# Graph kernel on one Trainium2 core: the twelve weight halves of the edge stage are loaded later in the aggregation loop, and split into high and low behind it

## The reference

```python
# x: (10000, 512); src, dst: (5000,) with dst sorted; edge_attr: (5000, 512)
# layer 0: graph convolution with self loops
out = segment_sum((x @ W)[src] * norm, dst) + b      # norm = dinv[src] * dinv[dst]
x = layernorm(x + leaky_relu(out))
# layer 1: attention over edges
r = concat([x[src], x[dst], edge_attr]) @ Wr.T + br
q, k, v = (x @ Wq.T + bq)[dst], r @ Wk.T + bk, r @ Wv.T + bv
m = v * segment_softmax(sum(q * k) / 8, dst)          # 8 heads of 64
out = x + segment_sum(m, dst) @ Wo.T + bo
out = (out - mean) / sqrt(var + eps) * gamma + beta   # mean, var over the nodes
x = layernorm(x + out)
```

## Time and profile before

| | us |
|---|---|
| median of 3 runs | 1425.84 (1417.3 to 1426.75) |
| the profiled execution's own time | 1421.64 |
| its span in the trace | 1419.9 |
| mean granted clock of TensorE | 0.976 of full |

### The profile page before, as it was taken

One profiled execution on the slowest core, in us unless ns is written; L12 is line 12 of the kernel. 1 busy time (PEld: TensorE's weight loads), 2 busy tenths in 40 slices (PEclk: granted clock), 3 DMA queues, 4 the chain that ended last, 5 costly groups with the idle time before them and its releaser, 6 DMA issues. The chain is left out here.

```text
span 1419.9 us, 22043 instructions
## 1 busy us (share of the span) xinstructions
PE 1336.9 (94%) x6660; PEld 1074.2 (76%) x6660; DVE 1092.5 (77%) x2043; ACT 592.8 (42%) x1107; POOL 827.0 (58%) x762
## 2 busy tenths in 40 slices
PE   7798889999999979999999999999999999859997
PEld 6677778888787858888888888888888888634443
DVE  6476647888888723788888888888888888868787
ACT  3466644555555511322222222222222223246786
POOL 3455515666666533566665666666666665558785
PEclk9999999999999979999999999999999999879999
DMA  8688775666666351444444444444444444759855
GB/s 287 216 290 295 242 238 182 222 222 221 220 214 228 141 160 45 120 130 133 132 135 134 132 130 132 133 134 134 134 134 134 134 134 118 261 185 363 291 194 186
DMA packets 128302, 257.97 MB, mean 182 GB/s; under 512 B 21459, under 2 KB 21907, under 8 KB 128114
## 3 DMA queue, kind: packets, MB, share of 16 engines
q1 hardware_dynamic: 97490, 175.31, 37.7%
q0 software_dynamic: 29920, 80.38, 18.2%
q10 hardware_dynamic: 832, 1.57, 0.3%
HBM read 197.18 MB, written 73.60 MB: 191 GB/s over the span
## 5 line engine op out<-in xcount | busy, mean ns | idle before, releaser
L207 PE MATMUL ps<-w_lo,w_hi 128*128 128x512 f32 (+2 forms) x1140 | 414.9, 364 | 6.9 <-DVE w_lo L1456 4.2
L208 PE MATMUL ps<-w_hi,w_lo 128*128 128x512 f32 (+2 forms) x1140 | 409.9, 360 | 0.0
L209 PE MATMUL ps<-w_hi 128*128 128x512 f32 (+2 forms) x1140 | 409.4, 359 | 0.0
L207 PEld LDWEIGHTS ps<-w_lo,w_hi 128*128 128x128 f32 x1140 | 216.5, 190 | 39.3 <-DVE w_lo L1456 5.6
L209 PEld LDWEIGHTS ps<-w_hi 128*128 128x128 f32 x1140 | 216.4, 190 | 32.1
L208 PEld LDWEIGHTS ps<-w_hi,w_lo 128*128 128x128 f32 x1140 | 216.7, 190 | 29.8
L1240 POOL TENSOR_TENSOR acc_x<-acc_x,node_rows 128x512 f32<-128x512 f32 x72 | 115.2, 1600 | 79.7 <-DMA node_rows<-x_table 75.5
L918 POOL TENSOR_TENSOR node_y<-node_z,node_x 128x512 f32<-128x512 f32 x79 | 102.2, 1293 | 98.3 <-issue 78.0
L209 PE MATMUL ps<-w_hi,agg_hi 128*128 128x512 f32 x316 | 125.3, 397 | 0.0
L207 PE MATMUL ps<-w_lo,agg_hi 128*128 128x512 f32 x316 | 125.3, 396 | 0.0
L208 PE MATMUL ps<-w_hi,agg_lo 128*128 128x512 f32 x316 | 125.2, 396 | 0.0
(11 more groups left out here) (266 smaller groups left out, 2943.9 us busy)
## 6 DMA issues: line engine op xcount, KB each, us to landing
node_x<-in_x SPq DMA_DIRECT2D x79, 256.0 KB
x_table<-node_x SPq DMA_DIRECT2D x79, 256.0 KB
node_rows<-x_table SPq DMA_DIRECT2D x79, 256.0 KB
coef_all<-coef_table SPq DMA_DIRECT2D x38, 512.0 KB
edge_part<-part SPq DMA_DIRECT2D x40, 256.0 KB
out_dram<-rows_over_w_lo SPq DMA_DIRECT2D x40, 256.0 KB
node_x<-in_ea SPq DMA_DIRECT2D x38, 256.0 KB
msg_table<-dst_rows_and_msg SPq DMA_DIRECT2D x38, 256.0 KB
```

The lines of the kernel that those rows point to most:

```text
L207: pe.matmul(to, left[0], right[1], start=first, stop=False)
L208: pe.matmul(to, left[1], right[0], start=False, stop=False)
L209: return pe.matmul(to, left[0], right[0], start=False, stop=last)
```

## The change

Nothing is removed or added: 12 ACT casts, 12 DVE subtractions and 10 loads change their places. The splits of halves 2 and 3 stay in turns 0 and 1. Those of halves 4 to 15 go into the last turn, half 4 ahead of the last sums on ACT, the rest between and behind the last edge tiles, the last six behind everything. The loads of halves 6 to 15 go from turns 0 to 9 into turns 6 to 15.

```diff
-LATER = 2 * (NW - 1)
@@ sync_program
-            if j + 6 < 2 * NW:
-                load_weights(j + 6)
+            if 6 <= j and j < 2 * NW:
+                load_weights(j)
@@ scalar_program, j == NB
                 part_rows(first)
+                weights_high(4)
                 sum_rows(2 * j - 2)
                 sum_rows(2 * j - 1)
                 high(third)
+                weights_high(5)
                 part_rows(second)
                 high(fourth)
+                for i in range(6, 8):
+                    weights_high(i)
                 part_rows(third)
+                for i in range(8, 10):
+                    weights_high(i)
                 part_rows(fourth)
+                for i in range(10, 2 * NW):
+                    weights_high(i)
                 continue
@@ scalar_program, end of a turn
-            if j < LATER:
+            if j < 2:
                 weights_high(j + 2)
@@ vector_program, j == NB
-                for t in ahead(j)[2:]:
-                    low(t)
+                third, fourth = ahead(j)[2:]
+                weights_low(4)
+                low(third)
+                weights_low(5)
+                low(fourth)
+                for i in range(6, 2 * NW):
+                    weights_low(i)
                 continue
```

## The result

The changed kernel takes 1428.28 us (median of 20 runs, 1425.16 to 1432.24), the kernel before in the same session 1424.3 (20 runs, 1417.1 to 1430.74). The ratio is **1.0032**, 95% interval 1.0019 to 1.0045: slower by about 4.6 us. The profiled execution took 1426.98 us with a span of 1425.2, so the spans differ by 5.3 us.

What follows compares the result with a forecast made beforehand. PE was taken to bound the kernel, the node stage outright, with waits for scans in the loop. From 1421.64 us, -10.6 (loop) + 6.2 (tail) + 1.6 (clock) = -2.8 gave 1419 us, range 1408 to 1430.

Steps and rivals of the forecast that it cites:

- The loop's gain: Aggregation loop, turns 2 to 13: without casts and subtractions, scans start earlier and PE waits less; 10.6 us gained.
- Loads on SP at nothing: Loop, turns 6 to 15: the ten moved loads' issue time on SP costs nothing and no cast waits for one.
- The tail: Behind the loop: DVE's moved subtractions decide when `node_agg` starts, at 216.3 instead of 210.15, 6.2 us later.
- The clock at the node stage's start: Start of the node stage: PE idle about 8.8 us instead of 2.65, so its lowered clock costs 1.6 us more.
- The zero of the Trainium skill's "TensorE: Matmul & The Clock Gate", Part 1: Rival at the node stage's start: a cold start costs the same however long PE rested, no added loss; 1417.2, chance 0.12.
- the transfers' 1429.4: Rival in turns 6 to 15: late loads make transfers set the pace, gain gone, tail still paid; 1429.4 us, chance 0.20.
- The gap of turn 2: Rival in the loop's turn 2: PE's idle gap and clock loss there, 8.4 us, go too; 1410.4 us, chance 0.14.

Runs made afterwards that it cites:

- e_splits_in_loop: Changed kernel with the splits kept in the loop (halves 6 to 15 in turns 9 to 18), none in the tail, loads late; ratio 1.0013 to the kernel before.
- e_loads_early: Changed kernel with its loads back in turns 0 to 9, splits still behind the loop; ratio 1.0049 to the kernel before, 1429.1 us.
- e_no_ea_loads: Changed kernel without the loads of the edge features from tile 15 on, old rows used again; ratio 1.0030 to the kernel before, 1426.6 us.
- e_plain_dinv: Changed kernel with the gather of `dinv` by index replaced by a plain DMA, factors of other rows; ratio 0.9921 to the kernel before, 1411.3 us.
- e_paced_after: Changed kernel with a wait on POOL so that at most four gathers stand in its queue; ratio 1.0014 to the kernel before, 1423.0 us.
- e_paced_before: Kernel before with a wait on POOL so that at most four gathers stand in its queue; ratio 0.9944 to the kernel before, 1412.5 us.

## Why the prediction was wrong, by its steps

- **The loop's gain, 10.6 us: the step that failed.** It measured 1.2. I took PE's recorded waits of the earlier trace rows, and the clock behind them, as time that goes with the splits behind which the scans stood, and left only the rate of turns 16 to 19. The runs show three things in its place. First, not all of the 12.2 us were the splits': with `dinv` by plain DMA the kernel before has 6.6 us of such waits, and at the place of the earlier trace rows the cast itself stood behind a `turn_back` whose completion came 2.9 us late. Second, these waits do go without hold-ups, 6.8 us up to turn 16, but then ACT waits for the stores of sums in one turn, 4.0 us, which leaves 2.8. That the freed engines meet another wait is what the prediction had no term for. Third, with hold-ups even the 2.8 comes to 1.2: their sum is 10.7 us larger than before, with longer idle times of PE and 3.2 us of clock behind them. The loops put that at less than 2 us net, by one profiled run each.
- **What stays open here**: why hold-ups come out worse without splits. Kernels with splits in the loop had 16.6 and 17.0 us of them, the six unpaced ones with these gathers and without splits 25.6 to 34.4. That POOL issues in longer runs is not the whole reason, since the kernel before has runs of eight too. Of all this the profile of before had a sign that I quoted and did not ask about: ACT's 2.21 us on "remote" in the earlier trace rows.
- **Loads on SP at nothing**: not refuted as the kernels are (e_splits_in_loop), probably wrong for a faster loop.
- **The tail, 6.2 us**: right. It measured 6.7, and 6.6 in the pair without hold-ups; DVE's subtractions decide, as forecast.
- **The clock at the node stage's start, 1.6 us**: the idle time was right, the size isn't shown. PE was idle 9.31 us (forecast about 9), then at 0.50 up to 222 us. The node stage is 0.9 us longer; but it varies as much from kernel to kernel, 275.1 to 276.5 us in the nine with twelve subtractions in the tail, 273.1 to 276.0 in the nine with four or none there. The zero of the Trainium skill's "TensorE: Matmul & The Clock Gate", Part 1, is neither confirmed nor refuted by that.
- **Rivals**: the transfers' 1429.4 came near the time by luck, by a mechanism that e_loads_early and e_no_ea_loads exclude for this kernel. The gap of turn 2 went only in the kernels without index gathers of `dinv` or with pacing (its turn 13.8 us before, 11.8 after, 5.4 in e_plain_dinv): there was a hold-up of 6.6 us in it. In e_paced_after a turn of 14.2 us follows right behind.
- **The time**: 1428.28 us lies between the 1408 and 1430 named, but not for the reason given: the forecast had the loop pay for the tail, and it did not.

## What to carry to other kernels

A wait that vanishes from a list is not yet time gained: ask what the waiting engine meets next, and sum the waits on "remote" and "issue" as well. When a row shows an engine late, ask what made the instruction before it late; in the earlier trace rows that was one entry further back. Work moved behind a loop is paid in full beyond the gap that is idle there (four subtractions were free here, twelve cost 6.7 us). An engine with 16% idle time is no free place when the piece put in is longer than the idle time of one step, and the piece can be slower there: 1.9 us, not 1.2. If gathers by index run beside matmuls, limiting how many are under way is worth a trial: one wait gave 8 us in the kernel before, no clear gain in the changed one, and a tighter one cost 68 us.

## What the runs showed of the hardware

PE's completions reached other engines up to 6.7 us behind its records before and 8.4 in e_paced_before, then in a burst 60 ns apart. Hold-ups of over 1 us came only with two gathers by index for each tile and more than two of them under way; what inside the chip does this was not tried. A gather by index occupies POOL for 1.26 us from start to start whatever it moves, 256 KB or 512 bytes. A subtraction of 128x1024 on DVE takes 1.20 to 1.23 us beside such gathers, and took 1.91 to 1.97 in all 24 cases in which POOL ran a TENSOR_TENSOR of 128x512 beside its first 0.8 to 0.9 us.
